# How far ahead the row maxima of a head are made, in the first causal attention of a decoder kernel

## What is computed

```python
q = layernorm((x @ Wq.T).reshape(B, S, H, hd).transpose(0, 2, 1, 3), q_gamma, q_beta)
k = layernorm(...)                                  # v is only projected
q = q * cos + rotate_half(q) * sin
k = k * cos + rotate_half(k) * sin
scores = scale * jnp.einsum('bhqd,bhkd->bhqk', q, k)
scores = jnp.where(mask, scores, -jnp.inf)          # mask: lower triangle
attn = jax.nn.softmax(scores, axis=-1)
out = jnp.einsum('bhqk,bhkd->bhqd', attn, v)
```

## Time and profile before

| | |
|---|---|
| median of three runs | 3107.12 us (3100.94 to 3112.64) |
| the profiled execution | 3109.32 us, of which the span of its instructions is 3107.6 us |
| PE (matmul) busy | 2918.1 us, 94% of the span |
| DVE busy | 2245.1 us, 72% |
| ACT busy | 1738.2 us, 56% |
| POOL busy | 532.6 us, 17% |
| mean granted clock of the PE | 0.962 of full speed |

### The profile page before, as it was taken

How to read it: one execution, slowest core, us unless ns; L and a number is a source line. 1 busy time by engine, 2 the same in 40 slices (tenths; PEclk the granted TensorE clock), 3 DMA queues, 4 the chain that set the end, 5 groups by cost and what they waited for, 6 DMA issues and landing times. The chain is left out here.

```text
span 3107.6 us, 94035 instructions
## 1 busy us (share of the span) xinstructions
PE 2918.1 (94%) x39187; PEld 1615.4 (52%) x39187; DVE 2245.1 (72%) x6174; ACT 1738.2 (56%) x2222; POOL 532.6 (17%) x730
## 2 busy tenths in 40 slices
PE   5999999999999999994999999999999999999998
PEld 2666666545655555552355555563333333356664
DVE  6788888577777777747688897327999999743114
ACT  2467667525555555563377777423677777741222
POOL 0255665130000000000222212302100000002330
PEclk8999999979999999997899999997999999999999
DMA  2433333310000001110311111203021121121112
GB/s 73 123 106 112 105 101 96 123 40 25 18 21 25 24 15 26 29 26 12 117 37 41 41 42 40 72 1 96 24 61 53 52 53 48 30 71 58 45 44 85
DMA packets 128328, 171.51 MB, mean 55 GB/s; under 512 B 45052, under 2 KB 98047, under 8 KB 126303
## 3 DMA queue, kind: packets, MB, share of 16 engines
q1 hardware_dynamic: 111296, 118.17, 13.8%
q0 software_dynamic: 11136, 46.76, 4.6%
q10 hardware_dynamic: 5472, 0.56, 0.1%
HBM read 122.76 MB, written 35.16 MB: 51 GB/s over the span
## 5 line engine op out<-in xcount | busy, mean ns | idle before, releaser
L502 PE MATMUL ps<-stack 96*32 96x401 bf16 (+5 forms) x13312 | 1220.3, 351 | 6.7 <-DVE mpart L679 1.8
L522 PE MATMUL ps<-stack 99*32 99x512 bf16 (+3 forms) x11648 | 1115.2, 369 | 54.0 <-ACT xT L431 24.4
L679 DVE TENSOR_REDUCE mpart<-ps 128x1 f32<-128x512 f32 (+2 forms) x1792 | 1031.4, 618 | 99.5 <-PE ps L502 82.3
L431 ACT ACTIVATE xT<-ps 128x1024 f32<-128x1024 f32 (+3 forms) x800 | 732.5, 938 | 387.2 <-PE ps L522 192.2
L431 ACT ACTIVATE cn<-ps 128x1024 f32<-128x1024 f32 (+4 forms) x800 | 686.6, 870 | 297.8 <-PE ps L522 148.4
L502 PEld LDWEIGHTS ps<-stack 96*32 96x32 bf16 x13312 | 470.7, 96 | 505.0 <-DVE mpart L679 196.5
L675 DVE CUSTOM_DVE_ANT_0 scrap<-ps,arena 128x401 bf16<-128x401 f32 (+1 forms) x1024 | 550.6, 575 | 156.6 <-PE ps L502 132.0
L522 PEld LDWEIGHTS ps<-stack 99*32 99x32 bf16 x11648 | 402.0, 97 | 400.3 <-issue 128.4
L552 PE MATMUL ps<-xT,vall 128*17 128x512 f32 (+4 forms) x3648 | 447.9, 503 | 1.1 <-POOL xT L384 1.0
L552 PE MATMUL ps<-cn,vall 128*17 128x512 f32 (+3 forms) x3392 | 430.6, 496 | 2.6 <-POOL cn L384 1.7
L530 PE MATMUL ps<-arena,big 128*32 128x512 fp8e4 (+1 forms) x3264 | 356.6, 382 | 0.0
(11 more groups left out here) (268 smaller groups left out, 2636.4 us busy)
## 6 DMA issues: line engine op xcount, KB each, us to landing
stack<-q_parts SPq DMA_DIRECT2D x384, 64.0 KB, 2.5
wbuf<-in_mask POOLq DMA_DIRECT2D x16, 800.5 KB, 4.7
stack<-k_parts SPq DMA_DIRECT2D x192, 64.0 KB, 2.7
wbuf<-in_maskT POOLq DMA_DIRECT2D x12, 1024.0 KB, 6.4
arena<-in_moe_w SPq DMA_DIRECT2D x19, 512.0 KB, 4.4
stack<-k_parts SPq DMA_DIRECT2D x192, 50.0 KB, 2.2
stack<-sums_inverse SPq DMA_DIRECT2D x16, 512.0 KB, 5.4
parts<-osb SPq DMA_DIRECT2D x240, 32.0 KB
```

The costliest lines, as they stand in the source:

```text
L431: nc.scalar.activation(e.prob[tile % P_SLOTS][0:rows, half * HALF + first:(half + 1) * HALF], S_PS(g)[0:rows, first:HALF], ACT.Exp, scale= ...
L502: last = nc.tensor.matmul(bank[quarter(j), 0:w], qs[b][0:KQ, t * P + 32 * j:t * P + 32 * j + 32], ks[b][0:KQ, a:a + w], start=True, stop=True)
L522: last = nc.tensor.matmul(S_PS(g)[quarter(j), lo:hi], ks[b][0:KM, kt * P + 32 * j:kt * P + 32 * j + 32], qs[b][0:KM, half * HALF + lo:half ...
L679: nc.vector.tensor_reduce(dst, src, AX, ALU.max).then_inc(unit_used, 1)
```

## The change

One number. Where `masks_ahead` is set, `lead` is 0.46 of the head's columns and no longer 0.36; the other three attentions keep theirs.

```diff
     width = [HALF - slot[3] for slot in slots]
-    lead = (0.36 if causal else 0.28 if not masked else 0.21) * sum(width)
+    lead = (0.46 if masks_ahead else 0.36 if causal else 0.28 if not masked else 0.21) * sum(width)
     turn = max(n for n in range(ns) if sum(width[n + 1:ns - 2]) >= lead)
```

## The result

The changed kernel takes 3091.77 us (median of 20 runs, 3085.52 to 3107.99) against 3108.41 us before (20 runs, 3100.94 to 3130.74). The ratio is 0.9948, with a 95% interval of 0.9933 to 0.9964: 16 us faster, give or take 5. The forecast was 3090. The border of 0.5%, up to which the prediction calls a change the same time, lies within the interval.

What follows compares the result with a forecast made beforehand. The PE has the least slack and waits 15.4 us for the row of maxima. Terms: -15.4 - 4.4 + 2.2 - 0.5 = -18.1 us, giving 3091.2 from the profile, 3089.0 from the median; taken as 3090 us, range 3081 to 3103.

Steps and rivals of the forecast that it cites:

- The chain starts earlier by 2.5 us, to a lead of 7.0.: First causal attention: the DVE's transpose of the maxima comes 2.5 us earlier, raising the lead from 4.5 to 7.0 us.
- All waits go, -15.4 us, one to one.: PE, first score matmul of a head: all 11 waits for the row of maxima vanish, saving 15.4 us in full.
- The longest of fifteen chains took 6.9: Transpose to first score matmul, first causal attention: no chain exceeded 6.9 us, so a lead of 7.0 us covers all.
- The clock, -4.4 us.: First causal attention: four half-clock dips behind waits of 1.61 us or more vanish, 1.1 us each, -4.4 us in all.
- The front, +2.2 us.: Before the first score: four more early units, 19 instead of 15, at the DVE's pace add 2.2 us.
- The tail, -0.5 us.: Period of head 14: four units fewer, moved to the front, at 0.14 us each, save 0.5 us.
- A period of 25.55 us throughout.: Heads of the first causal attention: a period is 25.55 us plus the wait, so 25.5 us throughout after the change.
- POOL's masks and the prefetch.: End of the first attention: POOL's masks start 2.2 us later, within 2 us of the prefetch, which costs nothing.
- The rival of the banks: Units sharing three PSUM banks stall the PE 2.7 us per head in 15 heads: slower, 3130 us; chance 0.05.
- the lead is bought only in part: Chain starts only 1 us earlier, or a new wait replaces it: gain 9.4 us, to 3098; chance 0.17.
- The dips stay: Clock dips in the first attention have another cause than waits and remain: gain 13.7 us, to 3093; chance 0.12.

Runs made afterwards that it cites:

- 0.28: The changed kernel with only its lead number edited, from 0.46 to 0.28: 1.0023 of before (1.0005 to 1.0041).
- the slow chain: The changed kernel (0.46) with the row of maxima stored and waited for three times over: 1.0174 of before (1.0126 to 1.0223).
- 0.40: The changed kernel with only its lead number edited, from 0.46 to 0.40: 0.9973 of before (0.9961 to 0.9985).
- 0.46 in both: The changed kernel with lead 0.46 in the second causal attention too, instead of 0.36: 0.9928 of before, 3087.7 us.

## Why the prediction was right

*The chain starts earlier by 2.5 us, to a lead of 7.0.* It was 6.7 us. Right, and so was where the row is needed.

*All waits go, -15.4 us, one to one.* Right in the main: none, 1.3 and 2.2 us were left in three profiles. The first of these was helped by luck, as it had only three slow chains; the other two had eight and seven. That a wait costs its own length, within 0.1 to 0.2 us, was shown from both sides, by the period of 27.08 us at 0.28 and by that of 28.20 in the slow chain. "The longest of fifteen chains took 6.9" was too small a sample: chains of 7.3 and 7.9 us came up later.

*The clock, -4.4 us.* The step was mis-sized. Waits bring dips: past head 0, none of the seven profiles whose waits stay below 1 us has one, and the slow chain, with a mean wait of 3.5 us in a head, spends 66 us of its heads at 1.2 GHz. But four dips behind these 15 us of waits were more than the usual. The second profile of the kernel before has one, so the mean of the two is 2.5 dips, 2.8 us at 1.1 each. Of that the changed kernel gives some back: in its first profile a dip of 6.8 us stands in head 0, whose period is 28.05 us there and 25.05 and 25.02 in its other two profiles, 3 us in one of three. So the term is nearer to 2 us than to 4.4. The Trainium skill (TensorE: Matmul & The Clock Gate, section "Why this matters for your kernels") warns only of longer gaps. It does not settle it for shorter ones, and the traces show that these can do it too: of the six waits of 1.6 to 2.4 us in the first profile four were followed by a dip, and of the three in the second, one.

The dips in head 0 are another matter, and the prediction had overlooked them. It says that the second causal attention has no dip in its 16 heads, but in the kernel before it has one of 3.41 us in head 0, which begins 1.3 us behind its first exponential (at 1551.29), and no wait for a row stands near it:

```profile
1552.59:1556.00 3.41, 3.41 (x36) 1.22 (x32) 2.19 (x5) 2.53 (x3) 0.38 (x2) 0.50 0.28 79
```

The second profile of before has the same at 1542.31. In the first attention such a dip stands in three of the six profiles with a lead of 0.40 or more and the units in their usual places (0.46, 0.40, 0.46 in both), and in none of the three at 0.36. Whether the longer front brings it there stays open.

*The front, +2.2 us.* It was 142.45 - 140.3 = 2.2, in two profiles. (Its upper bound of 2.8 was added up wrongly: three times 0.68 and 0.41 are 2.45.)

*The tail, -0.5 us.* This step failed. Nothing was won: head 14 takes 527.58 - 504.24 = 23.34 us, and took 23.45 less a wait of 0.12 ahead of the next head. It has its four units fewer, and does not end sooner; the runs do not show why.

*A period of 25.55 us throughout.* It became 25.63, and the kernel before had that already. Its head 1 has no wait for a row at either end, and takes 25.63 us, with the same work in it as the period shown above:

```profile
165.48:191.11 25.63, 25.01 (x506) 16.77 (x502) 22.65 (x62) 18.68 (x26) 11.80 (x11) 1.00 0.43 114
```

The 25.55 was worked out from heads that had a wait, less that wait, and the window of the earlier trace rows is no undisturbed period: it ends at 216.66, inside the wait from 215.93 to 218.33. So a wait for the row costs 0.08 us less than its length (the waits for the ACT, 9.4 us beside it and 11.4 without, fit that), and some 1 us of the 15.4 was not there to be won.

*POOL's masks and the prefetch.* POOL ended its masks at 553.5 us and SP sent the prefetch at 558.1; the prefetch did not wait for the masks, and from the last exponential to the first transpose of the next attention it took 105.3 to 106.0 us, against 104.9 and 105.3 before.

Together, the heads and the front gave 13 us by the profiles where 18 were forecast, and the runs gave 16 (11 to 21). That 3090 lies within 2 us of 3091.77 is partly luck: the clock, the tail and the waits were put some 5 us too high together, and the runs gained 3 us that the heads and the front do not show. The rival of the banks was wrong, and "the lead is bought only in part" as well. "The dips stay" was half right, in that there was less to win than its rival said.

## What to carry to other kernels

A small transfer that must be back in time should be given a lead by its slowest trips and not its median; the waits of one engine for it are what a trip is over the lead, and they cost nearly their full length where that engine is the bound. One profile is a small sample of such trips: they took up to 6.9 us in one and 7.9 in another. Look for what is large and runs beside it, for taking that away was worth as much as the lead. Once the lead covers the slowest trip, more of it buys nothing, and what is borrowed from the front is paid there, at the pace of the slower engine.

## What the runs showed of the hardware

- The granted clock of the front differs between executions of the same kernel: 31, 65 and 27 us at half in the three profiles of the changed kernel, which made the front 142.5, 157.2 and 142.5 us long. In the front of the second causal attention it was at half for 51 us in one profile of before and 68 in another (161.5 and 169.0 us), and for 65 to 82 in the three of the changed kernel. Single times of this kernel therefore say nothing below 20 us, and a phase is better compared by its own stretch and clock.
- The same chain, from the transpose to the landing of the row, takes 4.4 to 5.0 us with POOL's large loads taken out, and up to 7.9 us with them.
- It is slow when one of these loads is issued close to its start (between 2.1 us before the transpose and 2.4 us behind it, in all 68 of the 150 chains that took over 5 us), and not when such a load is merely under way. Either leg can be the slow one: 5.1 us from the transpose to SP's second send where 2.8 is usual, or 3.6 us from that send to the matmul.
- A dip of the granted clock can begin without any wait for a row, in head 0 of an attention: 3.41 us at 1552.59 in the kernel before.
